# The scan layer of a twelve-layer network: loads, projections, norms and bias adds placed elsewhere

## What is computed

```
x_n = ln(x, ln1_w, ln1_b)
phi_q = elu(x_n @ q_w + q_b) + 1
phi_k = elu(x_n @ k_w + k_b) + 1
lam = maximum(sigmoid(x_n @ dec_w + dec_b), 1e-8)
v_ext = concat([x_n @ v_w + v_b, 1])
out = forward scan (S = lam*S + k v) read by q, plus backward scan
attn = out[:K] / maximum(out[K:], 1e-6)
x = residual + (attn @ o_w + o_b)
return x + (gelu(ln(x, ln2_w, ln2_b) @ f1_w + f1_b) @ f2_w + f2_b)
```

## Time and profile before

| | us |
|---|---|
| median of three runs | 3258.06 |
| lowest, highest | 3256.76, 3258.07 |
| the profiled execution | 3254.58 |
| its span | 3252.5 |

### The profile page before, as it was taken

One profiled execution on the slowest core, in us unless ns is written; L12 is line 12 of the kernel. 1 busy time (PEld: TensorE's weight loads), 2 busy tenths in 40 slices (PEclk: granted clock), 3 DMA queues, 4 the chain that ended last, 5 costly groups with the idle time before them and its releaser, 6 DMA issues. The chain is left out here.

```text
span 3252.5 us, 43802 instructions
## 1 busy us (share of the span) xinstructions
PE 2875.6 (88%) x15996; PEld 1089.9 (34%) x16044; DVE 2296.2 (71%) x3000; ACT 1871.8 (58%) x3785; POOL 511.2 (16%) x832
## 2 busy tenths in 40 slices
PE   5999989899999997888968999999987899777788
PEld 2443434222222223533321222222255333253345
DVE  5454555899999994566649999999926766554951
ACT  2214322488888886456654888888846466554012
POOL 0000000200000100222221000110003222232630
PEclk9999999699999999899987999999999799988979
DMA  3210031300000000211012000000001211100000
GB/s 113 94 50 1 20 98 56 123 20 20 19 19 19 19 12 28 78 56 39 33 47 104 19 19 19 19 19 19 25 15 33 85 43 44 32 1 24 0 0 14
DMA packets 67506, 121.69 MB, mean 37 GB/s; under 512 B 16083, under 2 KB 42708, under 8 KB 64125
## 3 DMA queue, kind: packets, MB, share of 16 engines
q1 hardware_dynamic: 67292, 118.90, 11.3%
HBM read 95.38 MB, written 23.48 MB: 37 GB/s over the span
## 5 line engine op out<-in xcount | busy, mean ns | idle before, releaser
L1279 DVE TENSOR_REDUCE arena<-ps 128x1 f32<-128x1024 f32 (+7 forms) x1536 | 1573.1, 1064 | 239.6 <-PE ps L904 158.8
L1157 ACT ACTIVATE arena<-ps 128x512 f32<-128x512 f32 (+3 forms) x2816 | 1382.6, 573 | 406.9 <-PE ps L967 345.9
L898 PE MATMUL ps<-arena 61*128 61x512 bf16 (+4 forms) x2816 | 953.7, 384 | 67.0 <-DVE arena L1279 35.7
L967 PE MATMUL ps<-arena 64*128 64x512 bf16 (+4 forms) x2768 | 735.1, 371 | 66.4 <-ACT arena L1157 39.1
L924 PE MATMUL ps<-arena 128*32 128x512 f32 (+3 forms) x5632 | 712.9, 578 | 0.7 <-POOL arena L1238 0.3
L967 PEld LDWEIGHTS ps<-arena 64*128 64x128 bf16 (+1 forms) x2816 | 206.2, 95 | 769.1 <-ACT arena L1157 543.3
L898 PEld LDWEIGHTS ps<-arena 61*128 61x128 bf16 (+1 forms) x2816 | 259.3, 96 | 412.0 <-DVE arena L1279 356.6
L337 PE MATMUL ps<-xnT,moe_up 128*128 128x512 f32 x480 | 231.8, 608 | 0.0
L453 ACT ACTIVATE arena<-ps 128x512 f32<-128x512 f32 x120 | 71.4, 597 | 224.4 <-PE ps L337 224.4
L523 DVE TENSOR_TENSOR arena<-arena,ps 128x512 f32<-128x512 f32 x120 | 82.2, 687 | 158.2 <-ACT arena L453 129.7
L1207 POOL TENSOR_TENSOR arena<-arena,ones 16x128 bf16<-16x128 f32 x96 | 42.8, 446 | 845.1 <-ACT arena L1142 781.8
(11 more groups left out here) (228 smaller groups left out, 2703.4 us busy)
## 6 DMA issues: line engine op xcount, KB each, us to landing
arena<-m_w SPq DMA_DIRECT2D x32, 512.0 KB, 3.5
arena<-f_q SPq DMA_DIRECT2D x60, 144.0 KB
arena<-f_k SPq DMA_DIRECT2D x180, 48.0 KB
arena<-m_w SPq DMA_DIRECT2D x64, 128.0 KB, 3.9
arena<-in_w SPq DMA_DIRECT2D x4, 2048.0 KB
arena<-a_q SPq DMA_DIRECT2D x14, 576.0 KB
arena<-a_k SPq DMA_DIRECT2D x42, 192.0 KB
a_q<-arena SPq DMA_DIRECT2D x44, 96.0 KB, 2.0
```

The lines of the kernel that those rows point to most:

```text
L898: last = nc.tensor.matmul(at[:, k0 // CHUNK, 0:n], score_rows(Qop[par], j, slice(q0, q0 + P)), score_rows(Kop[par], j, slice(k0, k0 + n)), ...
L967: nc.tensor.matmul(ps[:, ring_bank(item), off:CHUNK], shifted_rows(Kop[par], j, slice(kb * P, (kb + 1) * P)), shifted_rows(Qop[par], j, sl ...
L1157: nc.scalar.activation(pr[:, (at % 2) * 4 + j, off:CHUNK], ps[:, ring_bank(item), off:CHUNK], ACT.Exp).then_inc(s.ex, 1)
L1279: nc.vector.tensor_reduce(mq[:, half, j * 4 + qb:j * 4 + qb + 1], src, AXX, ALU.max).then_inc(s.sread, 1)
```

## The change

- The weights of l3 are loaded by SP in the layer ahead, b1 (`load_scan_weights`), into the arena behind b1's own tile; their semaphore is waited for by PE after its first transposes and by POOL ahead of the scans. The biases come as a tile of 128 equal rows.
- The scans of batch 0 start after the projections of chunks 0 and 1. Their exps come first, then both sigmoids; chunks 2 and 3 are projected into other banks, with max(z+b, 0) made by ACT as a relu instead of DVE. Their features are finished by DVE after items 0 and 1, their decays after item 3.
- Batch 0's output projection is issued after gather(12), its sums and second statistics on DVE after item 13, and its second norm after item 14.
- POOL adds the two biases (to `res` after items 2 to 5, to `x` after items 6 to 9) and makes `x += res`; the matmuls with a row of ones are gone.
- DVE makes the last backward product with `phq` itself. The quotients of batch 1 come by chunk. Ups, downs and norms of the feed-forward part are in a written-out order, and the statistics for the next layer come one chunk earlier.

```diff
@@ binary_mlp, scan weights
-        def binary_mlp(tag, after):
+        def binary_mlp(tag, after, loads=None):
...
+            if loads:
+                part["sync"] = loads
...
+        scan_weights.at = 2 * FT * CHUNK
...
+        SCAN_LOADS = ((wq3, "wq3"), (wk3, "wk3"), (wd3, "wd3"), (wv3, "wv3"), (same3, "same"), (sel3, "sel"),
+                      (wo3, "wo3"), (bias3, "bias3"), (f13, "f13"), (f23, "f23"))
+        def load_scan_weights(sp):
+            for dst, name in SCAN_LOADS:
+                sp.dma_start(dst, a[name]).then_inc(scan_sem, 16)
@@ lion, tensor
+            Q_BANK, K_BANK, D_BANK = (1, 4, 1, 4), (2, 5, 2, 5), (3, 6, 7, 3)
+            OUT_BANK, UP_BANK, DOWN_BANK = (6, 7, 4, 5), (1, 6, 7, 2), (3, 4)
+                def project(ch):
+                    pe.wait_ge(s.xT, ch + 1)
...
+                        if ch >= 2:
+                            pe.wait_ge(s.ex, 2 * (ch - 2) + k + 1)
...
+                    if ch == 3:
+                        pe.wait_ge(s.sg, 1)
...
                 def value(n):
+                    if n == 0:
+                        pe.wait_ge(s.xT, CHUNKS)
+                        pe.wait_ge(s.ex, 5)
+                        pe.wait_ge(s.rl, 1)
+                    if n == 1:
+                        pe.wait_ge(s.ex, 6)
+                        pe.wait_ge(s.rl, 2)
+                        pe.wait_ge(s.sg, CHUNKS)
...
                 def gather(n):
+                    if n == 0:
+                        pe.wait_ge(s.sg, 3)
+                    if n == 1:
+                        pe.wait_ge(s.ex, 8)
+                        pe.wait_ge(s.rl, 4)
...
+                norm_tensor(pe, s, 0)
+                pe.wait_ge(scan_sem, 16 * len(SCAN_LOADS))
+                for ch in range(CHUNKS):
+                    project(ch)
+                    if ch + 1 < CHUNKS:
+                        norm_tensor(pe, s, ch + 1)
                 value(0)
                 value(1)
-                for n in range(18):
+                for n in range(17):
...
+                    if n == 12:
+                        out_project(0)
+                        out_project(1)
+                pe.wait_ge(s.bw, 17)
                 norm_tensor(pe, s, CHUNKS)
+                for f in range(3):
+                    up(0, f)
+                norm_tensor(pe, s, CHUNKS + 1)
+                gather(17)
+                up(0, 3)
+                for f in range(3):
+                    up(1, f)
+                out_project(2)
+                out_project(3)
+                up(1, 3)
+                down(0)
+                norm_tensor(pe, s, CHUNKS + 2)
+                down(1)
+                norm_tensor(pe, s, CHUNKS + 3)
+                for ch in range(2, CHUNKS):
+                    for f in range(FT):
+                        up(ch, f)
+                for ch in range(2, CHUNKS):
+                    down(ch)
@@ lion, scalar
+                def positive(ch, k):
+                    nc.scalar.activation(low[:, ch, k, :], ps[:, (Q_BANK, K_BANK)[k][ch], :], ACT.Relu,
+                                         bias=col(("l3_qb", "l3_kb")[k])).then_inc(s.rl, 1)
+                for ch in range(2):
+                    copy_turned(ch, "l3_g1", "l3_o1")
+                    exponent(ch, 0)
+                    exponent(ch, 1)
+                copy_turned(2, "l3_g1", "l3_o1")
+                decay(0)
+                decay(1)
+                for ch in range(2, CHUNKS):
+                    for k in range(2):
+                        exponent(ch, k)
+                        positive(ch, k)
+                    if ch == 2:
+                        copy_turned(3, "l3_g1", "l3_o1")
+                decay(2)
+                decay(3)
@@ lion, gpsimd
+                def add_bias(to, k, ch):
+                    at = to[:, ch * CHUNK:(ch + 1) * CHUNK].rearrange("p (n d) -> p n d", n=TPC)
+                    return nc.gpsimd.tensor_tensor(at, at, bias3[:, k, :].unsqueeze(1).to_broadcast([P, TPC, D]),
+                                                   ALU.add)
+                def add_residual(ch):
+                    pool.wait_ge(s.r, ch + 1)
+                    nc.gpsimd.tensor_tensor(x[:, r], x[:, r], res[:, r], ALU.add).then_inc(s.xr, 1)
...
+                    if 2 <= n < 2 + CHUNKS:
+                        pool.wait_ge(s.resid, n - 1)
+                        add_bias(res, 0, n - 2).then_inc(s.rb, 1)
+                    if 2 + CHUNKS <= n < 2 + 2 * CHUNKS:
+                        last = add_bias(x, 1, n - 2 - CHUNKS)
...
+                    if n == 13:
+                        norm_gpsimd(pool, s, t, CHUNKS)
+                        norm_gpsimd(pool, s, t, CHUNKS + 1)
+                    if n in (15, 16):
+                        add_residual(n - 15)
@@ lion, vector
+                def add_out(ch):
+                    dve.wait_ge(s.y, ch + 1)
+                    dve.wait_ge(s.rb, ch + 1)
+                    nc.vector.tensor_tensor(res[:, r], res[:, r], ps[:, OUT_BANK[ch], :], ALU.add)\
+                        .then_inc(s.r, 1)
+                    norm_stats(dve, s, t, res_rows(ch), CHUNKS + ch)
+                def second_norm(ch):
+                    k = CHUNKS + ch
+                    dve.wait_ge(s.tp, k - 1)
+                    norm_apply(dve, s, res_rows(ch), lambda n: xn[:, k % 2, n, :], k).then_inc(s.xn, 1)
                 for n in range(18):
                     scans(n)
+                    if n == 0:
+                        feature(2, 0)
+                        feature(2, 1)
+                    if n == 1:
+                        feature(3, 0)
+                        feature(3, 1)
+                    if n == 3:
+                        decay(2)
+                        t.settle(dve, decay(3))
...
+                    if n == 13:
+                        add_out(0)
+                        add_out(1)
+                    if n == 14:
+                        second_norm(0)
+                        second_norm(1)
+                dve.wait_ge(s.bw, 18)
+                nc.vector.tensor_tensor(bw[:, 17 % 3, :], bw[:, 17 % 3, :], phq[:, SEQ:2 * SEQ], ALU.mult)\
+                    .then_inc(s.blast, 1)
+                quotients(slice(2 * CHUNK, 3 * CHUNK), slice(4, 5), 18)
+                quotients(slice(3 * CHUNK, 4 * CHUNK), slice(5, 6), 18)
+                add_out(2)
+                add_out(3)
+                second_norm(2)
+                second_norm(3)
```

More of the change, by code:

```diff
@@ L1880, in lion @@
             oT = c(TOKENS)
[L1881 to L1889, removed]
@@ L1896, in tensor @@
                     pe.wait_ge(s.xT, ch + 1)
                     t = slice(ch * CHUNK, (ch + 1) * CHUNK)
[L1898 to L1901, removed]
+                    for k, (w, bank) in enumerate(((wq3, Q_BANK[ch]), (wk3, K_BANK[ch]))):
+                        if ch >= 2:
+                            pe.wait_ge(s.ex, 2 * (ch - 2) + k + 1)
+                        nc.tensor.matmul(ps[:, bank, :], w, xnT[:, t], start=True, stop=True)\
@@ L1931, in gather @@
                                          start=e in (0, 8), stop=False, skip_group_check=True)
-                    pe.wait_ge(s.bq, n + 1)
+                    if n < 17:
+                        pe.wait_ge(s.bq, n + 1)
+                    else:
+                        pe.wait_ge(s.blast, 1)
                     for h in range(2):
@@ L1947, in tensor @@
                     gather(n)
[L1948 to L1956, removed]
-                        last = nc.tensor.matmul(at, ones[0:1, :], rowo[0:1, 0:D], start=False, stop=True)
-                    last.then_inc(s.y, 1)
@@ new lines, in positive, with decay @@
+                def positive(ch, k):
+                    nc.scalar.activation(low[:, ch, k, :], ps[:, (Q_BANK, K_BANK)[k][ch], :], ACT.Relu,
+                                         bias=col(("l3_qb", "l3_kb")[k])).then_inc(s.rl, 1)
+                def decay(ch):
+                    act.wait_ge(s.pj, 3 * ch + 3)
+                    nc.scalar.activation(lam[:, ch * CHUNK:(ch + 1) * CHUNK], ps[:, D_BANK[ch], :],
+                                         ACT.Sigmoid, bias=col("l3_db")).then_inc(s.sg, 1)
@@ L2049, in vector, with positive, feature @@
                 t = Tally(s.vec)
+                def positive(ch, k):
+                    dve.wait_ge(s.pj, 3 * ch + k + 1)
+                    nc.vector.tensor_scalar(low[:, ch, k, :], ps[:, (Q_BANK, K_BANK)[k][ch], :],
+                                            col(("l3_qb", "l3_kb")[k]), 0.0, ALU.add, ALU.max)\
+                        .then_inc(s.mn, 1)
+                def feature(ch, k):
+                    tt = slice(ch * CHUNK, (ch + 1) * CHUNK)
+                    dst = (phq, phk)[k]
+                    dve.wait_ge(s.ex, 2 * ch + k + 1)
+                    if ch >= 2:
+                        dve.wait_ge(s.rl, 2 * (ch - 2) + k + 1)
+                    return nc.vector.scalar_tensor_tensor(dst[:, tt], dst[:, tt], 1.0, low[:, ch, k, :],
```

(1 more changed line is left out.)

226 lines of the change are left out of this document (115 added, 111 removed).

## The result

The median fell from 3258.07 us (3256.76 to 3259.6, four runs) to 3213.7 us (3213.0 to 3216.87, four runs), a ratio of 0.9866 with an interval of 0.9848 to 0.9883. That is 44.4 us between the medians and 41.0 between the profiled executions (3254.58 and 3213.57). The forecast was 37 and 3221. The last DVE add of l3 comes 40.0 us earlier; b2 behind it takes 57.0 instead of 57.7.

A forecast was written before the change was run, and what follows sets the result against it. DVE was taken to bound l3's scans, with chains of waits before them and PE behind. Last add at 3116.4+41.0 = 3157.4 against 3194.8 saved 37.4 us, giving 3220.7, said as 3221; range 3210 to 3234.

The forecast's parts named there:

- The lock: Rival, chance 0.12: DVE keeps the shared port and POOL pays; 6 us back in the scans, time 3212.
- the low clock: Rival, chance 0.12: PE runs at low clock in the tail, 12 us of its work doubles, time 3233.
- values: Rival, chance 0.04: value(0) and value(1) wait behind ACT work, batch 1's projections stay before the scans; some 15 us, 3236.
- the slower rival: Rival, chance 0.02: POOL's bias adds delay multiplies; slower overall above 5.6 us an add, 3269 at 7.0.
- The bound on the span from the first scan to E: Sign: first scan to last scan end (E) near 143 us, otherwise the prediction is wrong.
- Loads: Start of l3: weight loads hidden under b1 let PE's first transposes come 8.3 us earlier.
- S: Head of l3: first scan at 2973.8, 23.7 us earlier, with only batch 0's two chunks ready.
- S1: Second item's scan: at 2984.3, 17.6 us earlier, set by value(0) at 2984.2 and chunk 2's features at 2984.3.
- Scans: From S1 to last scan end: work added on DVE sums to 17.5 us over 114.6, so E at 3116.4.
- the second norm of two chunks is 8x0.34 less overlap: 2.3: Scans on DVE: batch 0's second norm adds 2.3 us of the 17.5.
- Tail: Last scan end (E) to last DVE add (X): PE bound, 41.0 us against 78.3 before.
- Eight halves at the down rate of 1.09: PE work in the tail: 16 down tiles at 1.09 us each, 17.4 in all.

The follow-up runs named there:

- second execution: The kernel after, unchanged, profiled again on another chip; 3215.36 us, ratio to before 0.9869.
- ones_rows: Kernel after with biases added by matmuls of a ones row on PE again and POOL's eight bias adds gone; median 3240.01 us, ratio 0.9942.
- all_together: Kernel after with reciprocal on ACT, chunk 0's and 1's norms late, early chunk 3 features, floors on POOL, later x biases; 3195.04 us, ratio 0.9804.

## Why the prediction was right, and where its terms were off

**Direction and size.** The forecast held: 37.4 expected, 41.0 between the profiled executions. None of the rivals came. The lock was not cheap (3.64 and 3.09), the low clock did not return in the tail (1.00), values were not late by loads, and POOL's bias add took 1.3 where the slower rival needed 5.6. The bound on the span from the first scan to E, near 143, came out at 146.6, and at 143.9 in the second execution.

**Loads.** 8.3 predicted, 8 to 10 measured by removal and by return. The layer has five table loads instead of nine, as said; the groups by line of after show two for exp and two for sigmoid (the fifth is gelu's) and relu with none:

```profile
L2058 ACT ACTIVATE arena<-ps,cols 128x512 f32<-128x512 f32 x4 | 2.7, 682 | 0.0
...
L2054 ACT ACT_TABLE_LOAD x2 | 2.6, 1283 | 0.0
L2063 ACT ACT_TABLE_LOAD x2 | 2.6, 1283 | 0.0
```

By "ScalarE: Activation LUTs" of the Trainium skill (Table sets) relu was to need no load, and the trace agrees (0.68 each, no load).

**Head.** S came 16.6 behind b1 against 18.4 predicted: I had counted both projections at the low clock, and only the first was slow (PE took 3.65 for the first four matmuls at L1910 and 1.98 for the next four). S1, which lies behind the values, came 0.7 early. The second execution had 27.4 from b1 to S1 against 28.1. That S1 fits so well is in part luck. The prediction had two bounds for it, and one never came: the features of chunk 2 were to be held by POOL until 2984.3, but they ended at 2977.7, since POOL's first multiply began only at 2979.5. PE alone set S1, and there the late projection and the values took 7.6 us from 2976.04 instead of the 6.4 counted (granted clock 0.50 from 2976 to 2980), but began 1.8 earlier.

**Scans.** 17.5 more predicted, 20.5 measured. Features 3.6 (3.9 predicted), floors 3.1 (3.4), item 13 7.5 (6.9) and item 9 2.0 or 0.6 (1.0) were sized about right. The step that failed is "the second norm of two chunks is 8x0.34 less overlap: 2.3". I applied the turns to features and floors but not to the eight applies of the norm, which read SBUF alone as well; they took 4.25 and waited out the POOL multiply at 3097.65. The step's right form is one POOL multiply of some 2 on top of its own length, as for the others. "SBUF — State Buffer" of the Trainium skill (SBUF: two separate sides) speaks of a lock held for a whole instruction; the 3.64, 3.09 and 4.25 agree with it, and the 6.63 shows that waiting can last for two instructions beyond the one in flight.

**Tail.** 41.0 predicted, 36.1 measured, in both executions of after. Two terms of the sum were mis-sized. "Eight halves at the down rate of 1.09" took the length from the earlier trace rows, where each eight are followed by a ones row; there 1.50 from start to start is 0.93 for the halves and 0.57 for the ones row, not 1.09 and 0.41. That is 2.6 over 16 down tiles and 0.4 in the output projections. The allowance of 1.9 for a low clock was not needed in this stretch. By the same reading the ones rows were worth more than I gave them, which the run with them back showed from the other side (19.6 against 11 to 15).

**Total.** Errors of +3 in the scans, -5 in the tail and -1 in the head leave 3 us in b1 to X; b2 was 0.7 shorter. The other 3 between the 41.0 and the 44.4 is where the profiled execution of before lies under its median: 3.5, while after's lies 0.1 under. That is the spread of single executions, and b1's end alone varies by 7. So the nearness of the total is luck in part: scans that came out long and a tail that came out short nearly cancel.

**Left open.** Why item 9 goes one way or the other was seen, not steered. Of the 40 us, the early start of the scans and the new order of the tail were never taken out alone. PE's short stretch at the low clock in the ones_rows tail was not explained. That the reciprocal on ACT keeps PE's clock high in item 13 rests on one kernel with that change alone; all_together, which has it too, shows no slow group there either. A pause of PE of other length was not tried.

## What to carry to other kernels

When an early start of one engine's stretch feeds work into another engine that is full, count each added operation there at the price it has beside its neighbour, not at its price alone: here the two features and two floors cost 6.7 us beside POOL's multiplies and 2.05 when POOL was idle. Moving work ahead of a bottleneck is paid back only if it is work the bottleneck needn't do: batch 0's sums and norms cost 11.1 us in the scans and saved 5.8 behind them. Compare single profiles item by item, and only where the edit can act: three sums of differences against one profile promised 17 us, the items 10, and 10.5 came. And read a matmul's length from start to start of like groups: a small matmul between large ones can cost more than its own bar.

## What the runs showed of the hardware that I had not expected

A one-row matmul of 128 columns (two halves, busy 0.48) lengthened a tile of eight 128-row halves from 0.93 to 1.51 us, two thirds of what the eight cost. A DVE scan waited for two POOL operations in a row, beyond the one in flight (6.63 instead of 2.3), in one execution and took turns in another of the same program. And the reciprocal of 1024 columns, 6.55 us on DVE, is two ACT operations of 1.06 and two table loads of 1.28 at most, 4.7 together, on an engine that had nothing else to do.
